# Second cross attention begun inside the block of the rotary projection, in the rotations' buffers

## The chip, the cores and the metric

The kernel runs on one core of a Trainium2 chip. The metric is device time in microseconds (us) of one execution of the whole program; lower is better. Five instruction streams run beside each other and meet only at semaphores: TensorE (PE: matmuls, and PEld: its weight loads), VectorE (DVE), ScalarE (ACT), GpSimd (POOL) and SyncE (SP), which issues most of the DMA transfers.

## The reference

Two layers work on x, 16 batches of 64 rows of 256. Each layer is a cross attention against a context of 128 keys per batch, a self attention and a feed-forward stage. The cross attention of the second layer, whose start is changed, is this (16 heads, latent width 192, key width 64):

```python
q_hk  = (hidden_q @ Wq.T).reshape(b, s, H, K)
q_big = jnp.einsum('bshk,hkq->bshq', q_hk, w_kc_q)     # then rotated by position in this layer
q_r   = jnp.einsum('bshq,hqr->bhsr', q_big, W_qr)
k_r   = jnp.einsum('bld,hdr->bhlr', kv_rope, W_kr)
attn  = softmax(einsum('bhsr,bhlr->bhsl', q_r, k_r))
ctx_c = einsum('bhsl,bld->bhsd', attn, kv_rope)
out   = einsum('bhsd,hkd->bshk', ctx_c, w_kc_kv).reshape(b, s, H * K) @ Wo.T
```

## The kernel before

Every stage is a function that opens a block: an area of the program in which each engine has its own instruction list, written out by hand, and at whose end all engines meet. Buffers that a block allocates are free again after it. The order of work on an engine is the order in its list; nothing is rescheduled.

**Projection, `cross_project_rotary` (L1498).** The queries are made in 24 steps k: four quads of four heads, each for two halves of the batches (half 0 is batches 0 to 7, half 1 is 8 to 15; the pair is a unit, so there are units 0 to 7), three chunks of the latent each. Per step, PE makes two products `big(k, 0)` and `big(k, 1)`, DVE multiplies each by a table of cosines or sines (`rotate`, L1769: two 128x1024 products, into `times_a[k % 2]` and `times_b[k % 2]`), POOL adds the two (L1553, into `turned[k % 3]`), and PE folds the sum into the latent banks 6 and 7 (`fold(k)`, L1644 and L1652), two steps behind its own `big`. After the third chunk of a unit, ACT rounds the query to fp16 (`high`, L1714) and DVE subtracts for the low part (`low`, L1780, which counts the semaphore `q_lo` up by 4 a unit). ACT and POOL also split weights of the coming self attention in the last six steps (`split_rotary_*`, `split_output_*`, four slices of the output weight at L1828 and L1835). The last two folds, the last `high` and the last `low` come after the loop.

**Attention, `cross_attention` (L584), used by both layers.** A block of its own, with its own buffers. It walks over tiles of two batches; `j` is the batch whose scores are made, `b` the one two batches behind. For one batch:

- PE `score(j)` (L643): 16 matmuls into two banks of one pair (pairs alternate with j);
- DVE `neg_max` (L800): two reductions, one for each half of the heads (q = 0, 1);
- ACT `exponentials` (L717): eight activations that also give the row sums, four for each q;
- DVE `invert` (L771): one reciprocal for each q;
- POOL normalises the probabilities (L753), one instruction for each q, and copies the keys (L749);
- PE `turn` (L640) transposes them, DVE copies them out (`probs_t`, L786), PE `mix` (L658) multiplies by the keys, ACT rounds (`ctx_hi`, L730), DVE subtracts (`ctx_lo`, L775); after two batches PE `output` (L672) makes the output product, DVE adds it to x (L810).

On DVE the order within batch j is: copy of turn q = 0, invert(j-1, 0), `ctx_lo`, copy of turn q = 1, invert(j-1, 1), then the two maxima of j. So maxima of j are queued behind the last reciprocal of j-1, which waits for the last exponential of j-1.

Of the kernel before, what the change touches and what calls it, by code (L numbers as in the profile page):

```python
# [14 lines left out]
ALU = mybir.AluOpType  # L15
# [7 lines left out]
P = 128  # L23
# [7 lines left out]
BH = B // 2  # L31
# [326 lines left out]
def cross_project_plain(nc, g):  # L358
# [4 lines left out]
    with ExitStack() as own:  # L363
# [185 lines left out]
        def _(dve):  # L549
# [31 lines left out]
            pair_loop(step)  # L581


def cross_attention(nc, g, tag, weights=None):  # L584
# [13 lines left out]
    HP = PAIRS // 2  # L598
    with ExitStack() as own:  # L599
        def sb(name, shape, dt):  # L600
            return own.enter_context(nc.sbuf_tensor(f"{tag}_{name}", shape, dt))

        probs = [sb(f"probs{u}", [P, PAIRS, L], F32) for u in range(2)]
        probs_t = [sb(f"probs_t{u}", [P, PAIRS, P], F32) for u in range(2)]
        keys = [sb(f"keys{u}", [P, DC], F32) for u in range(2)]
        ctx_hi = [sb(f"ctx_hi{v}", [P, PAIRS, 2, S], F16) for v in range(2)]
        ctx_lo = [sb(f"ctx_lo{v}", [P, PAIRS, 2, S], F16) for v in range(2)]
        neg_max = [sb(f"neg_max{u}", [P, PAIRS], F32) for u in range(2)]
        total = [sb(f"total{u}", [P, PAIRS], F32) for u in range(2)]
        inverse = [sb(f"inverse{u}", [P, PAIRS], F32) for u in range(2)]  # L610
        scored, maxed, exped = g.sem(f"{tag}_scored"), g.sem(f"{tag}_maxed"), g.sem(f"{tag}_exped")
        inverted, normed = g.sem(f"{tag}_inverted"), g.sem(f"{tag}_normed")
        turned, turn_kept = g.sem(f"{tag}_turned"), g.sem(f"{tag}_turn_kept")
        keys_kept = g.sem(f"{tag}_keys")
        mixed, mix_high, mix_kept = g.sem(f"{tag}_mixed"), g.sem(f"{tag}_mix_high"), g.sem(f"{tag}_mix_kept")
        out_done, added = g.sem(f"{tag}_out"), g.sem(f"{tag}_added")

        ln = normalise_steps(nc, g, f"{tag}_ln", groups=[(2 * q, 2 * q + 2) for q in range(TILES // 2)])
        score_bank = [[g.bank[k][:].rearrange("p (n l) -> p n l", n=HP) for k in banks]
                      for banks in ((0, 1), (6, 7))]  # L620
        turn_bank = [g.bank[k][:].rearrange("p (n l) -> p n l", n=HP) for k in (2, 3)]
        mix_bank = g.bank[4][:]
        out_bank = [g.bank[k][:, 0:D] for k in (5,) * (TILES - 2) + (0, 1)]
        mix_view = mix_bank.rearrange("p (n s) -> p n s", n=PAIRS)
        block = own.enter_context(nc.Block())

        SCALED = (5, 7)

        def tile_loop(eng, step):
            for i in range(TILES + 3):  # L630
                step(i, i % 2, i < TILES, 1 <= i <= TILES, 2 <= i <= TILES + 1)

        @block.tensor
        def _(pe):
            def turn(b, u):
                for q in range(2):
                    pe.wait_ge(normed, 2 * b + q + 1)
                    wait(pe, turn_kept, 2 * b + q - 1)
                    for n in range(HP):
                        mm = nc.tensor.transpose(turn_bank[q][:, n, :], probs[u][:, q * HP + n, :], m.ident[:])  # L640
                    mm.then_inc(turned, 1)

            def score(j, u):  # L643
                for q in range(2):
                    wait(pe, exped, 2 * j + q - 3)
                    for n in range(HP):
                        at = 2 * (q * HP + n)
                        lhs = m.q_stack[:, j, at:at + 2, :]
                        mm = accumulate(nc, score_bank[u][q][:, n, :],
                                        [(lhs, m.kvt_hi[:, j, :]), (lhs, m.kvt_lo[:, j, :])])  # L650
                    mm.then_inc(scored, 1)

            def mix(b, u):
                pe.wait_ge(turn_kept, 2 * b + 2)
                pe.wait_ge(keys_kept, b + 1)
                wait(pe, mix_kept, b)
                for e in range(2):
                    mm = nc.tensor.matmul(mix_view[e * DC:(e + 1) * DC], keys[u][:],  # L658
                                          probs_t[u][:, :, e * S:(e + 1) * S], start=True, stop=True)
                mm.then_inc(mixed, 1)  # L660

            def output(t, u):
                v = t % 2
                if u == 0:
                    pe.wait_ge(mix_kept, 2 * t + 2)
                    if t < TILES - 2:
                        wait(pe, added, t)
                for n in range(u * HP, (u + 1) * HP):
                    hi, lo = (c[v][:, n, :, :].rearrange("p b s -> p (b s)") for c in (ctx_hi, ctx_lo))
                    factors = split_factors(hi, lo, m.out_hi[:, n, :], m.out_lo[:, n, :])  # L670
                    for k, (lhs, rhs) in enumerate(factors):
                        mm = nc.tensor.matmul(out_bank[t], lhs, rhs, start=(n == 0 and k == 0),  # L672
                                              stop=(n == PAIRS - 1 and k == len(factors) - 1))
# [1918 lines left out]
```

## Time and profile before

| what | value |
|---|---|
| time, median of 3 runs | 779.67 us (778.89 to 780.49) |
| the profiled execution's own time | 774.19 us |
| span of the profiled execution | 772.4 us |
| mean granted TensorE clock | 0.954 |
| PE, DVE, ACT, POOL busy | 89%, 76%, 54%, 50% of the span |
| changed seam: last `low` of the projection to first score of the attention | about 415 us from the span's start |

A timeline row gives the start, the duration (of a merged run of instructions, where x is over 1), the engine, the line, what is written and read, and in brackets how long the engine stood idle before it and what released it. A windows row gives for a stretch the busy time of each engine and the clock that was granted to TensorE (1.00 is 2.4 GHz, 0.50 is 1.2 GHz).

### The profile page before, as it was taken

What the parts mean: (1) busy time and instruction counts of PE and PEld (TensorE: products, weight loads), DVE (VectorE), ACT (ScalarE), POOL (GpSimd) and SP (SyncE); (2) the same over time, 40 slices, a digit from 0 to 9 for tenths busy, and PEclk for the clock granted to TensorE, in tenths of its full rate; (3) what the DMA queues carried; (4) which work ended last, traced back from release to release, by engine and by line L of the source; (5) the groups of instructions that cost most, each with busy time, mean ns of one, the idle gap of its engine ahead of it and who ended that gap; (6) DMA issues with size and microseconds to landing.
All of it is one profiled execution on the core that took longest, in us unless ns stands there. A gap on an engine that the chain in (4) does not pass through costs nothing. (4 is left out here: it accounts for less than half of the span.)

```text
span 772.4 us, 15774 instructions
## 1 busy us (share of the span) xinstructions
PE 685.5 (89%) x5490; PEld 462.7 (60%) x5490; DVE 584.1 (76%) x1149; ACT 418.9 (54%) x1317; POOL 384.8 (50%) x338
## 2 busy tenths in 40 slices
PE   5997899998767489999995999889999999999987
PEld 4664677687424354445333677567777776767754
DVE  4466789765788765757684899897888888889787
ACT  2565778654358422222335878255555656566575
POOL 1503555473146324434485555356576687777512
PEclk9998899998579589999998999999999999999999
DMA  6465000000110041710010000023331221211001
GB/s 195 132 188 220 1 3 1 1 2 1 59 38 1 0 140 38 239 54 1 1 41 1 2 2 2 1 62 98 117 111 46 62 62 44 62 43 42 2 0 57
DMA packets 33576, 41.97 MB, mean 54 GB/s; under 512 B 15073, under 2 KB 23265, under 8 KB 32609
## 3 DMA queue, kind: packets, MB, share of 16 engines
q1 hardware_dynamic: 33504, 41.06, 17.4%
q8 instruction: 40, 0.66, 0.3%
q14 instruction: 32, 0.25, 0.1%
HBM read 40.00 MB, written 1.05 MB: 53 GB/s over the span
## 5 line engine op out<-in xcount | busy, mean ns | idle before, releaser
L2140 POOL TENSOR_TENSOR ra_direct<-ra_direct,ra_crossed 128x512 f32<-128x512 f32 x64 | 81.2, 1270 | 73.6 <-DVE ra_crossed L2326 73.5
L717 ACT ACTIVATE c_probs<-bank,c_neg_max 128x128 f32<-128x128 f32 x256 | 91.2, 382 | 29.4 <-DVE c_neg_max L800 29.4
L2326 DVE SCALAR_TENSOR_TENSOR ra_crossed<-bank,ra_bias,ra_sin 64x512 f32<-64x512 f32 x128 | 96.0, 750 | 1.9
L753 POOL TENSOR_TENSOR c_probs<-c_probs,c_inverse 128x512 f32<-128x512 f32 x64 | 66.6, 1041 | 61.1 <-DVE c_inverse L771 61.1
L1553 POOL TENSOR_TENSOR r_turned<-r_times_a,r_times_b 128x1024 f32<-128x1024 f32 x24 | 56.4, 2351 | 70.6 <-DVE r_times_b L1769 70.6
L2275 ACT ACTIVATE ra_probs_t<-bank 64x256 f32<-64x256 f32 x64 | 24.2, 378 | 60.4 <-PE bank L2214 60.1
L717 ACT ACTIVATION_READ_ACCUMULATOR c_probs<-bank,c_neg_max 128x1 f32 x256 | 56.5, 221 | 0.0
L2283 ACT ACTIVATE ra_probs<-ra_masked,ra_neg_max 128x64 f32<-128x64 f32 x128 | 42.9, 336 | 20.0 <-DVE ra_neg_max L2346 19.7
L1850 POOL TENSOR_TENSOR ra_w_lo<-ra_raw,ra_w_hi 128x768 f16<-128x768 f32 x32 | 52.7, 1647 | 0.0
L58 PE MATMUL bank<-xt_hi,ra_w_hi 128*128 128x512 f16 x128 | 49.1, 384 | 0.9 <-PEq L599 0.9
L58 PE MATMUL bank<-xt_hi,ra_w_lo 128*128 128x512 f16 x128 | 49.0, 383 | 0.0
L58 PE MATMUL bank<-xt_lo,ra_w_hi 128*128 128x512 f16 x128 | 49.0, 383 | 0.0
L2326 DVE SCALAR_TENSOR_TENSOR ra_direct<-bank,ra_bias,ra_cos 128x512 f32<-128x512 f32 x64 | 47.5, 743 | 1.0 <-PE bank L58 0.7
L786 DVE COPY c_probs_t<-bank 128x512 f32<-128x512 f32 x64 | 43.8, 684 | 5.6 <-PE bank L640 5.2
L2374 DVE SCALAR_TENSOR_TENSOR ra_z_lo<-bank,ra_v_bias,ra_z_hi 128x512 f16<-128x512 f32 x32 | 23.9, 748 | 29.4 <-ACT ra_z_hi L2296 29.4
L640 PEld LDWEIGHTS bank<-ident_sb,c_probs 128*128 128x128 f32 x256 | 28.6, 145 | 28.4 <-issue 21.1
L58 PE MATMUL bank<-ra_w_hi,xt_hi 128*128 128x128 f16 x256 | 44.9, 220 | 0.0
L58 PE MATMUL bank<-ra_w_lo,xt_hi 128*128 128x128 f16 x256 | 44.9, 220 | 0.0
L58 PE MATMUL bank<-ra_w_hi,xt_lo 128*128 128x128 f16 x256 | 44.9, 220 | 0.0
L800 DVE TENSOR_REDUCE c_neg_max<-bank 128x4 f32<-128x512 f32 x64 | 40.9, 678 | 2.6 <-PE bank L58 2.5
L58 PE MATMUL bank<-kvt_hi,l_q_stack 128*128 128x128 f16 x256 | 35.8, 233 | 7.5 <-PEq L1508 4.5
L640 PE MATMUL bank<-ident_sb,c_probs 128*128 128x128 f32 x256 | 36.9, 287 | 3.6 <-POOL c_probs L753 3.6
(271 smaller groups left out, 2082.0 us busy)
## 6 DMA issues: line engine op xcount, KB each, us to landing
ra_raw<-l_attn_w_dram SPq DMA_DIRECT2D x32, 384.0 KB, 3.0
wq<-l_wq_dram SPq DMA_DIRECT2D x16, 256.0 KB, 2.8
wo<-l_wo_dram SPq DMA_DIRECT2D x16, 256.0 KB, 3.4
wkcq<-l_wkcq_dram SPq DMA_DIRECT2D x16, 192.0 KB, 2.8
ra_wo<-l_attn_wo_dram SPq DMA_DIRECT2D x1, 2048.0 KB, 10.7
wqr<-l_wqr_dram SPq DMA_DIRECT2D x16, 96.0 KB, 2.3
wkv<-l_wkv_dram SPq DMA_DIRECT2D x16, 64.0 KB, 2.8
x_res<-x_dram SPq DMA_DIRECT2D x2, 512.0 KB, 5.6
```

Of the source, the lines that this page charges most:

```text
L58: mm = nc.tensor.matmul(out, lhs, rhs, start=(n == 0), stop=(n == last))
L640: mm = nc.tensor.transpose(turn_bank[q][:, n, :], probs[u][:, q * HP + n, :], m.ident[:])
L717: e = nc.scalar.activation(probs[u][:, n, :], score_bank[u][q][:, n - q * HP, :], ACT.Exp, bias=neg_max[u][:, n:n + 1], accum_out=total[u] ...
L753: nc.gpsimd.tensor_tensor(out=probs[u][:, at, :], in0=probs[u][:, at, :], in1=inverse[u][:, at].unsqueeze(2).broadcast_to([P, HP, L]), op= ...
L786: nc.vector.tensor_copy(probs_t[u][:, at, :], turn_bank[q]).then_inc(turn_kept, 1)
L800: nc.vector.tensor_reduce(neg_max[u][:, at], score_bank[u][q], AX.X, ALU.max, negate=True).then_inc(maxed, 1)
L1553: nc.gpsimd.tensor_tensor(out=turned[k % 3][:], in0=times_a[k % 2][:], in1=times_b[k % 2][:], op=ALU.add).then_inc(rotated, 1)
L1850: nc.gpsimd.tensor_tensor(out=m.ra_w_lo[f][:], in0=m.ra_raw[f % 2][:], in1=m.ra_w_hi[f][:], op=ALU.subtract).then_inc(g.ra_split, 1)
L2140: nc.gpsimd.tensor_tensor(out=direct[e][k][:], in0=direct[e][k][:], in1=crossed[k][:], op=ALU.add).then_inc(roped, 1)
L2275: ins = nc.scalar.activation(probs_t[at, :, b, :], turn_bank[at].rearrange("p (a s) -> p a s", a=TH), ACT.Copy)
L2283: ins = nc.scalar.activation(probs[1 - e][:, t, :], masked[1 - e][:, t, :], ACT.Exp, bias=neg_max[1 - e][:, t:t + 1], scale=-1.0, accum_ou ...
L2326: ins = nc.vector.scalar_tensor_tensor(dst[out_lo:out_lo + rows].rearrange("p t (b s) -> p (t b) s", b=2), src[lo:lo + rows], bias[e][lo:l ...
```

## The change

The attention becomes a set of steps, `cross_attention_steps`, that can be put into another block. The first layer uses it as before in a block of its own (with a few waits more on PE, on semaphores that have passed). In the second layer the block is gone: the projection's block runs the attention's steps on each engine.

- PE: `score(0)` before fold 22, `score(1)` before fold 23 (both need only half 0 of the queries), then the rest from the turn of batch 0.
- ACT: the eight exponentials of batch 0 before the last two `high`, then the rest from batch 1.
- DVE: the maxima of batch 0 after the last rotation; then the attention's list, with the last `low` of side 0 after the maxima of batch 1 and that of side 1 after the maxima of batch 2.
- POOL: the fourth slice of `split_output_low` moves from behind the last rotation to behind the normalising of batch 1.
- Buffers: the probabilities, their transposes and the contexts lie in the rotations' buffers. Banks: scores (3, 4) and (0, 1), turns 2 and 5, mix 6, output 7. PE waits for the last `low` of side 0 before the first mix (bank 6) and for that of side 1 before the first output (bank 7).

```diff
-def cross_attention(nc, g, tag, weights=None):
+def cross_attention_steps(nc, g, own, tag, banks, ready, room=None, weights=None):
...
+    even, odd, turns, mixes, outs = banks
+    ln = normalise_steps(nc, g, f"{tag}_ln", groups=[(2 * q, 2 * q + 2) for q in range(TILES // 2)],
+                         banks=odd + (6, 7))
...
+    queries, first_ready, all_ready = ready
...
+    def score(pe, j):
+        u = j % 2
+        if j in (0, BH):
+            pe.wait_ge(queries, first_ready if j == 0 else all_ready)
...
+        def mix(b, u):
+            pe.wait_ge(turn_kept, 2 * b + 2)
+            pe.wait_ge(keys_kept, b + 1)
+            wait(pe, mix_kept, b)
+            if b == 0 and begun:
+                pe.wait_ge(queries, all_ready - 2)
...
+                if t == 0:
+                    pe.wait_ge(queries, all_ready)
...
+                if head and j >= begun:
+                    score(pe, j)
...
+                if head and j >= begun:
+                    exponentials(act, j, 0)
...
+                for q in range(2):
+                    at = slice(q * HP, (q + 1) * HP)
+                    pool.wait_ge(inverted, 2 * j + q + 1)
+                    nc.gpsimd.tensor_tensor(
+                        out=probs[u][:, at, :], in0=probs[u][:, at, :],
+                        in1=inverse[u][:, at].unsqueeze(2).broadcast_to([P, HP, L]),
+                        op=ALU.mult).then_inc(normed, 1)
+                if u == 0 and i in SCALED:
+                    ln.rstd(pool, SCALED.index(i))
+                between(j)
...
+                if head and j >= begun:
+                    peak(dve, j)
+                if i < 2:
+                    between(j)
...
@@ -1537,7 +1581,20 @@
+        room = {"probs": [sb("probs0", [P, PAIRS, L])[:], wide(times_a[0])],
+                "probs_t": [wide(times_b[0]), wide(times_a[1])],
+                "ctx_hi": contexts(times_b[1]), "ctx_lo": contexts(turned[0])}
         ln = g.ln1
+        att = cross_attention_steps(nc, g, own, "c1", ((3, 4), (0, 1), (2, 5), 6, 7), (q_lo, 4 * (UNITS - 1), 4 * UNITS),
+                                    room)
...
-                elif at >= 2:
+                elif 2 <= at < PER_QUAD - 1:
                     split_output_low(nc, g, pool, at - 2)
+
+            def between(j):
+                if j == 1:
+                    split_output_low(nc, g, pool, 3)
+
+            att.gpsimd(pool, between)
...
-            for k in (STEPS - 2, STEPS - 1):
+            for j, k in enumerate((STEPS - 2, STEPS - 1)):
+                if j == 1:
+
+                    pe.wait_ge(multiplied, 2 * STEPS - 1)
+                att.score(pe, j)
                 fold(k)
+            pe.wait_ge(multiplied, 2 * STEPS)
+            att.tensor(pe, 2)
...
+            for q in range(2):
+                att.exponentials(act, 0, q)
             for side in range(2):
                 high(UNITS - 1, side)
+            att.scalar(act, 1)
...
-            for side in range(2):
-                low(UNITS - 1, side)
+            att.peak(dve, 0)
+
+            def between(j):
+                if j in (1, 2):
+                    low(UNITS - 1, j - 1)
+
+            att.vector(dve, 1, between)
+    return att.ln
...
-            cross_project_rotary(nc, g)
-            ln = cross_attention(nc, g, "c1")
+            ln = cross_project_rotary(nc, g)
```

## Rows read from the trace of the kernel before

**Rows 1.** The page: span, and busy time, share and instructions of each engine.
```profile
span 772.4 us, 15774 instructions
PE 685.5 (89%) x5490; PEld 462.7 (60%) x5490; DVE 584.1 (76%) x1149; ACT 418.9 (54%) x1317; POOL 384.8 (50%) x338
```

**Rows 2.** Windows: stretch, length, busy PE, PEld, DVE, ACT, POOL; clock; DMA share, GB/s.
```profile
404.00:410.00 6.00, 3.28 (x10) 1.15 (x12) 1.66 (x2) 0.00 (x0) 6.00 (x4) 1.00 0.00 0
...
415.00:420.00 5.00, 3.45 (x34) 3.31 (x35) 1.75 (x5) 4.19 (x17) 1.28 (x2) 0.72 0.02 5
...
435.00:440.00 5.00, 5.00 (x49) 3.77 (x47) 4.29 (x9) 4.16 (x24) 2.92 (x4) 1.00 0.02 5
```

**Rows 3.** Timeline of PE at the seam.
```profile
403.59 0.38 PE L58 MATMUL bank<-xt_hi,r_big_lo 128*128 128x512 f16 x1
404.31 1.98 PE L1652 MATMUL bank<-r_turned,r_fold_outer 128*128 128x512 f32 x4 [0.34 <-POOL r_turned L1553]
408.70 1.93 PE L1644 MATMUL bank<-r_turned,r_fold_inner 64*64 64x512 f32 x8 [2.40 <-POOL r_turned L1553]
415.10 0.27 PE L58 MATMUL bank<-kvt_hi,l_q_stack 128*128 128x128 f16 x1 [4.46 <-PEq L1508]
```

**Rows 4.** Timeline of DVE at the seam.
```profile
401.86 1.41 DVE L1780 TENSOR_TENSOR l_q_stack<-bank,l_q_stack 64x512 f16<-64x512 f32 x2
...
404.44 1.21 DVE L1769 TENSOR_TENSOR r_times_b<-bank,r_table_b 128x1024 f32<-128x1024 f32 x1
411.92 2.85 DVE L1780 TENSOR_TENSOR l_q_stack<-bank,l_q_stack 64x512 f16<-64x512 f32 x4 [6.27 <-ACT l_q_stack L1714]
```

**Rows 5.** Timeline of POOL at the seam and in batches 1 and 2.
```profile
406.30 2.35 POOL L1553 TENSOR_TENSOR r_turned<-r_times_a,r_times_b 128x1024 f32<-128x1024 f32 x1
408.59 2.14 POOL L1835 TENSOR_TENSOR ra_wo_lo<-ra_wo,ra_wo_hi 128x1024 f16<-128x1024 f32 x1
...
423.80 1.04 POOL L753 TENSOR_TENSOR c_probs<-c_probs,c_inverse 128x512 f32<-128x512 f32 x1 [0.36 <-DVE c_inverse L771]
...
426.80 1.04 POOL L753 TENSOR_TENSOR c_probs<-c_probs,c_inverse 128x512 f32<-128x512 f32 x1 [1.16 <-DVE c_inverse L771]
```

**Rows 6.** Timeline of ACT: seam, then the first exponential of batches 0, 1, 2, 3, 8.
```profile
410.68 2.44 ACT L1714 ACTIVATE l_q_stack<-bank 64x512 f16<-64x512 f32 x4 [8.42 <-PE bank L1644]
415.06 1.28 ACT L717 ACT_TABLE_LOAD   x1 [1.93 <-PEq L1508]
416.87 0.37 ACT L717 ACTIVATE c_probs<-bank,c_neg_max 128x128 f32<-128x128 f32 x1 [0.53 <-DVE c_neg_max L800]
...
420.60 0.37 ACT L717 ACTIVATE c_probs<-bank,c_neg_max 128x128 f32<-128x128 f32 x1 [0.82 <-DVE c_neg_max L800]
...
424.35 0.37 ACT L717 ACTIVATE c_probs<-bank,c_neg_max 128x128 f32<-128x128 f32 x1 [0.84 <-DVE c_neg_max L800]
...
428.59 0.37 ACT L717 ACTIVATE c_probs<-bank,c_neg_max 128x128 f32<-128x128 f32 x1 [0.85 <-DVE c_neg_max L800]
...
449.75 0.37 ACT L717 ACTIVATE c_probs<-bank,c_neg_max 128x128 f32<-128x128 f32 x1 [0.84 <-DVE c_neg_max L800]
```

**Rows 7.** Lines of 425 to 475 us: busy, mean ns, idle before and its releaser.
```profile
L717 ACT ACTIVATE c_probs<-bank,c_neg_max 128x128 f32<-128x128 f32 x95 | 33.9, 383 | 9.2 <-DVE c_neg_max L800 9.2
```

**Rows 8.** Timeline of DVE from the maxima of batch 2 to those of batch 3.
```profile
423.63 1.27 DVE L800 TENSOR_REDUCE c_neg_max<-bank 128x4 f32<-128x512 f32 x2
425.94 0.69 DVE L786 COPY c_probs_t<-bank 128x512 f32<-128x512 f32 x1 [1.03 <-PE bank L640]
...
427.89 1.26 DVE L800 TENSOR_REDUCE c_neg_max<-bank 128x4 f32<-128x512 f32 x2
```

**Rows 9.** Windows: the start of the first layer's attention.
```profile
73.10:83.20 10.10, 8.68 (x55) 6.15 (x53) 5.76 (x12) 7.57 (x41) 4.55 (x6) 0.50 0.00 1
```

**Rows 10.** Timeline of ACT there: first exponential of batches 2 and 3.
```profile
81.38 0.37 ACT L717 ACTIVATE c_probs<-bank,c_neg_max 128x128 f32<-128x128 f32 x1 [0.84 <-DVE c_neg_max L800]
86.37 0.37 ACT L717 ACTIVATE c_probs<-bank,c_neg_max 128x128 f32<-128x128 f32 x1 [1.42 <-DVE c_neg_max L800]
```

More of the change, by code:

```diff
@@ new lines, in sb, with taken @@
+    def sb(name, shape, dt):
+        return own.enter_context(nc.sbuf_tensor(f"{tag}_{name}", shape, dt))
+    def taken(name, count, shape, dt):
+        return room[name] if room and name in room else [sb(f"{name}{u}", shape, dt)[:] for u in range(count)]
+    probs = taken("probs", 2, [P, PAIRS, L], F32)
+    probs_t = taken("probs_t", 2, [P, PAIRS, P], F32)
+    keys = [sb(f"keys{u}", [P, DC], F32) for u in range(2)]
+    ctx_hi = taken("ctx_hi", 2, [P, PAIRS, 2, S], F16)
+    ctx_lo = taken("ctx_lo", 2, [P, PAIRS, 2, S], F16)
@@ new lines, in gpsimd, with step @@
+    def gpsimd(pool, between=lambda j: None):
+        def step(i, v, head, middle, tail):
+            if not head:
+                return
+            for u in range(2):
+                j = 2 * i + u
+                wait(pool, mixed, j - 1)
+                nc.gpsimd.tensor_copy(keys[u][:], m.kv2[:, j, 0, :]).then_inc(keys_kept, 1)
+                for q in range(2):
+                    at = slice(q * HP, (q + 1) * HP)
[7 more added lines that the diff above has]
+                between(j)
+        if weights:
+            weights.fill_ones(pool)
+        tile_loop(step)
+        ln.rstd(pool, 2)
@@ L625, in cross_attention @@
+    att = Fields()
+    att.score, att.exponentials, att.peak, att.ln = score, exponentials, peak, ln
+    att.tensor, att.scalar, att.gpsimd, att.vector = tensor, scalar, gpsimd, vector
+    return att
+def cross_attention(nc, g, tag, banks, ready, weights=None):
+    with ExitStack() as own:
+        att = cross_attention_steps(nc, g, own, tag, banks, ready, None, weights)
         block = own.enter_context(nc.Block())
[L627 to L631, printed above, removed]
@@ L653, in mix @@
[L653 to L673, printed above, removed]
-                if u == 1:
-                    mm.then_inc(out_done, 1)
@@ L690, in step @@
-            def step(i, v, head, middle, tail):
-                for u in range(2):
-                    j, b = 2 * i + u, 2 * i + u - 2
-                    if middle:
-                        turn(b, u)
-                    if head:
-                        score(j, u)
-                    if u and tail and i < TILES + 1:
-                        output(i - 2, 0)
-                    if not u and 3 <= i < TILES + 2:
-                        output(i - 3, 1)
-                    if middle:
-                        mix(b, u)
-                    if middle and not head:
-                        pe.wait_ge(exped, 2 * B - 1 + u)
-                        ln.transpose(pe, u)
-                    if u and i == TILES + 1:
-                        last_output()
@@ L722, in step @@
-            def step(i, v, head, middle, tail):
-                for u in range(2):
-                    j, b = 2 * i + u, 2 * i + u - 2
-                    if head:
-                        exponentials(j, u, 0)
-                    if middle:
-                        act.wait_ge(mixed, b + 1)
-                        wait(act, out_done, i - 2)
-                        nc.scalar.activation(ctx_hi[1 - v][:, :, u, :], mix_view, ACT.Copy).then_inc(mix_high, 1)
-                    if head:
-                        exponentials(j, u, 1)
-                    if middle and not head:
-                        ln.high(act, u)
```

320 lines of the change are left out of this document (177 added, 143 removed).

## The prediction

> **What bounds the kernel now.** I began with the page. TensorE is busy for 89% of the span and no other engine for more than 76% [rows 1], which says little of a seam between two stages. So I read windows around it: of the 6 us from 404 us on PE works 3.28, DVE 1.66 and ACT nothing (only POOL is busy), while in the steady attention PE fills its window entirely [rows 2]. The seam is a chain of waits, and I read it engine by engine from the timelines.
>
> The chain is: POOL makes the last rotated sum until 408.65 [rows 5]; PE folds it, 408.70 to 410.63 [rows 3]; ACT rounds the last queries, 410.68 to 413.12 [rows 6]; DVE makes their low parts, 411.92 to 414.77 [rows 4]; then all engines meet at the end of the block and the first score starts at 415.10 [rows 3]. The first exponential comes at 416.87 [rows 6], because a maximum lies before it. The table load at 415.06 (1.28 us) is over at 416.34 and costs nothing [rows 6]. All the while batches 0 to 7 have been ready: their last low part, of unit 6, ends at 403.27 [rows 4]. That is the slack which the change can reach, from the front.
>
> What sets the pace behind the seam decides whether a head start is kept. The first exponentials of batches 3 and 8 lie 21.16 us apart [rows 6], 4.23 us a batch. Between 425 and 475 us all of the 9.2 us for which the exponentials waited were ended by the maxima [rows 7]. So the pace is a loop: exponentials of j, reciprocal, maxima of j+1 (queued behind it on DVE), exponentials of j+1. The loop has no tie to a fixed point in time, and no transfer is in it. PE's work fits into this period, but only just [rows 2].
>
> **The change, step by step.** I follow one marker, the first exponential of batch 3, since from there on the loop repeats. It stands at 428.59 now [rows 6].
>
> *Scores 0 and 1.* PE issues its last `big` product at 403.59 and waits 0.34 us for fold 22 [rows 3]. In the window from 415 on, the 32 matmuls of two scores and two more take 3.45 us [rows 2], so a score is at most 1.7 us at a mostly low clock; from 404 to 410 the clock is 1.00 [rows 2], and my estimate there is half of it, 0.9 us. Score 0 runs at about 403.9 to 404.8, fold 22 moves behind it by some 0.6 us and ends at about 406.9, score 1 is done before 408. Fold 23 waits for POOL until 408.65 in any case, after 2.40 us of idle time [rows 3]. Both scores are hidden in that idle time; without it they would cost 1.8 us, and with the low clock they would push fold 23 by 0.6 us. Score 1 needs bank 1, whose rotation is the one before that of 404.44, so it is free by then [rows 4]. Price: nothing.
>
> *Maxima and exponentials of batch 0.* DVE is idle for 6.27 us after the last rotation (404.44 + 1.21 = 405.65) [rows 4]: maxima until 406.9. ACT is idle for 8.42 us before 410.68 [rows 6]. The table load fits ahead of the first exponential (ACT is free from 410.68 - 8.42 = 402.26), the eight exponentials take 2.9 us (batch 0 begins at 416.87, and batch 1 begins at 420.60 after 0.82 us of idle time [rows 6]: 419.78 less 416.87). They run at about 406.4 to 409.3, before the last fold ends at 410.63. `high` starts at 410.68 as before. Price: nothing; if the cover were gone, `high` would be late by what they pass 410.68; there are 1.4 us to spare. The copies behind exponentials need no new table load: the attention has this mix already, and its starts are evenly 4.23 us apart [rows 6].
>
> *Batch 1.* Its maxima are queued behind the reciprocals of batch 0 (409.4), and end at about 410.7, before `low` of side 0 can start at 411.92 [rows 4]. Its exponentials come behind `high` on ACT: 413.1. POOL normalises batch 0 from 408.65 on; it no longer has the fourth slice (2.14 us) there [rows 5]. PE turns batch 0 and makes score 2 by 412.7.
>
> *Batch 2.* Now batch 1 starts at 420.60 and batch 2 at 424.35, 3.75 us later [rows 6]. Nothing in that step is new: reciprocal 1, then maxima 2. 413.1 + 3.75 = 416.85, which is **7.50 us earlier** than 424.35.
>
> *Low part of side 1.* It stands on DVE behind the maxima of batch 2, and the copy of turn 1, the reciprocals and maxima of batch 3 are queued behind it. The maxima of batch 2 end 0.55 us after the marker of batch 2 (423.63 + 1.27 = 424.90 against 424.35) [rows 6, 8], so at 417.4. Half of the 2.85 us row [rows 4] is 1.43: 418.8. From the copy to the start of the maxima of batch 3 it is 1.95 us (425.94 to 427.89), and 0.70 from there to the exponential (428.59) [rows 6, 8]: 418.8 + 1.95 + 0.70 = 421.45. Without it, the loop would give 416.85 + 4.24 = 421.09. So it costs about 0.4 of its 1.43 us, and the rest takes the place of 1.03 us for which DVE waits there now [rows 8]. The mix of batch 0 waits for the low part of side 0, which ends at about 413.3; the copies that it also needs come after it. The output of tile 0 comes two batches later.
>
> *Fourth slice on POOL.* The second normalising of batch 1 starts 3.20 us after that batch's marker (423.80 against 420.60) [rows 5, 6]: 416.3 to 417.3; the slice 2.14 us [rows 5]: 419.5. Behind it on POOL is the key copy and the first normalising of batch 2, now 2.45 us after its marker (426.80 against 424.35) [rows 5, 6], which would be 419.3, and about 419.5 with DVE's delay above. So it is late by 0.2 us, and PE's turn waits for it; DVE's copy of that turn comes only after the maxima of batch 3, about 422.0. Bounds: 0 and 2.14; I take 0, by the rows, since the turn is ready before DVE is.
>
> *The first layer.* It gets three waits on PE for semaphores that have passed, tens of ns at the most; and a block end goes, which is in the marker's way already (414.77 to 415.10). Price: nothing.
>
> **Sum:** 428.59 - 421.45 = **7.1 us**. Against the profiled execution's 774.19 that is 767.1. It lies 5.5 us below the median of 779.67. Nothing on the seam's chain is a transfer or differs by chance as far as these rows show, so I take the 7.1 us from the median as well: **772.6**, 0.9% less.
>
> **TensorE's clock.** At the seam PE idles 4.46 us [rows 3], and the window from 415 on has a mean clock of 0.72, that is partly 1.2 GHz [rows 2]. In the first layer, the attention's start runs wholly at 0.50 for 10 us, busy for 8.68 of 10.10 us [rows 9], and there batches 2 and 3 are 4.99 us apart (86.37 less 81.38) and not 4.23 [rows 10]: the low clock costs 0.76 us, once. Here the 4.46 us gap goes, but PE becomes sparse between 412.7 and 421 (turn, mix and one score each in some 4 us). The Trainium skill (TensorE: Matmul & The Clock Gate, Part 4: PE-mode transpose) says that transposes do not count as busy time for the clock gate; by it half of that work would not count, and the sum would be 7.1 - 0.8 = 6.3 us. No row here separates transposes from other matmuls. I take 0, because the gap that precedes the low clock now is gone, and keep 0.8 as a rival.
>
> **Rivals.**
> - *The clock falls in the sparse start* and costs what it costs in the first layer, 0.76 us: 773.4. For it: the first layer's start [rows 9, 10]. Against: the long gap is gone, and the loop is set by ACT and DVE, so only a PE that is very late shows. The skill's sentence on transposes stands on this side.
> - *The moved pieces queue wholly*: the low part with 1.43 instead of 0.4, and the slice with 2.14 us. 7.5 - 1.43 - 2.14 = 3.9: 775.8. For it: both stand in the loop's lists. Against: the idle 1.03 us before the copy, and POOL's idle 1.16 us before the normalising [rows 5, 8].
> - *The head start is given back or the seam was hidden*: 779.7. It would need something behind the seam that is bound to a fixed time, a transfer for instance. The timeline of ACT and its releasers show none [rows 6, 7].
> - *Slower: TensorE stays at 1.2 GHz in the steady attention.* PE's work fills its window at full clock [rows 2], so a batch would take up to twice 4.23, 4.2 us more. Two such batches eat the 7.1 us, three make it 12.7 - 7.1 = 5.6 us slower: 785.3. Trigger: the clock falls in the sparse start and doesn't rise. Against: in the first layer it rose by itself after 83.2, before the outputs begin, since PE at the low clock was busy nearly all the time [rows 9].
>
> **How the numbers follow.** Forecast 0.65, clock 0.18, queueing 0.10, no gain 0.04, slower 0.03. About 0.2% (1.6 us) is what a measurement of this kernel can tell from no change. Faster by more than that: the first three, 0.93; within it 0.04; slower 0.03. The range starts at 779.67 less 7.5 (the low part free) less 1.6 for the scatter of the runs (they span 1.6 us): 770.5. It goes up to 776.0, which takes in the clock and the queueing case (775.8), and leaves out the last two, 0.07. What is left of the 0.2 is for prices that I have not thought of.
>
> **What would show it.** Right: score 0 and 1 between the last `big` and fold 23; exponentials of batch 0 before the last `high`, which stays at 410.7; batch 1 at 413.1, batch 2 near 416.9, batch 3 near 421.5, then 4.23 us a batch; the last low part of 1.43 us between maxima 2 and the copy of turn 1. Wrong: fold 23 or `high` later than now; a second table load; batch 3 later than 422.2 (clock) or 423.5 (queueing); the period above 4.23; a stage after the attention that is longer than before.

## The result, and the profile after

| | before | changed |
|---|---|---|
| time, median | 779.28 us (16 runs, 775.5 to 783.81) | 770.53 us (16 runs, 767.58 to 776.13) |
| ratio | 1 | 0.9895, 95% interval 0.9872 to 0.9918 |
| the profiled execution | 774.19 us, span 772.4 | 769.27 us, span 767.4 |

The ratio means 8.2 us less (6.4 to 10.0). Forecast were 7.1 us less and a time of 772.6 us; measured were 770.53. A second series of the same two kernels gave a ratio of 0.9906 (0.9874 to 0.9938), which is 7.3 us.

The two spans differ by 5.0 us only, and that is not the size of the effect at the seam. The last rotation of the projection ends at 405.65 us in the trace of before [rows 4] and at 407.80 in the changed one: 2.15 us that lie ahead of the seam. That is scatter: in three traces of the kernel before, this point lies anywhere between 405.65 and 411.13 us. So everything below is measured from the end of the last rotation (T), up to the first product of the self attention, 493.02 before and 488.75 after. That stretch went from 87.37 to 80.95 us, 6.42 us less. What follows it took 279.38 and 278.65 us.

PE in the changed kernel:

```profile
405.73 0.38 PE L58 MATMUL bank<-xt_hi,r_big_lo 128*128 128x512 f16 x1
405.95 0.22 PE L58 MATMUL bank<-kvt_hi,l_q_stack 128*128 128x128 f16 x1
...
406.84 1.94 PE L1715 MATMUL bank<-r_turned,r_fold_outer 128*128 128x512 f32 x4
408.62 0.22 PE L58 MATMUL bank<-kvt_hi,l_q_stack 128*128 128x128 f16 x1
...
410.86 1.93 PE L1707 MATMUL bank<-r_turned,r_fold_inner 64*64 64x512 f32 x8 [1.18 <-POOL r_turned L1610]
412.72 1.09 PE L657 MATMUL bank<-ident_sb,r_probs 128*128 128x128 f32 x8
...
417.65 1.08 PE L667 MATMUL bank<-r_times_b,c_keys 128*64 128x512 f32 x4 [2.94 <-DVE r_times_b L805]
...
423.08 1.63 PE L667 MATMUL bank<-r_times_a,c_keys 128*64 128x512 f32 x4 [1.94 <-DVE r_times_a L805]
424.64 1.97 PE L657 MATMUL bank<-ident_sb,r_probs 128*128 128x128 f32 x8
```

Score 0 takes 0.89 us (405.95 to 406.84) and stands between the last `big` and fold 22 (L1715). Score 1 begins at 408.62, behind fold 22. Fold 23 (L1707) still waits for POOL, now for 1.18 us and not 2.40 [rows 3], so both scores are hidden. The turn of batch 0 follows at once. The names `r_times_b`, `r_times_a` and `r_probs` are only the new places of the attention's data, in the projection's block.

ACT in the changed kernel: table load, first exponential of batch 0, the last `high`, first exponentials of batches 1, 2, 3, 4 and 9:

```profile
404.42 1.28 ACT L727 ACT_TABLE_LOAD   x1
408.43 0.37 ACT L727 ACTIVATE r_probs<-bank,c_neg_max 128x128 f32<-128x128 f32 x1 [2.73 <-DVE c_neg_max L781]
...
412.84 2.44 ACT L1783 ACTIVATE l_q_stack<-bank 64x512 f16<-64x512 f32 x4 [1.51 <-PE bank L1707]
415.31 0.37 ACT L727 ACTIVATE r_times_a<-bank,c_neg_max 128x128 f32<-128x128 f32 x1
...
419.04 0.37 ACT L727 ACTIVATE r_probs<-bank,c_neg_max 128x128 f32<-128x128 f32 x1 [0.84 <-DVE c_neg_max L781]
...
423.72 0.37 ACT L727 ACTIVATE r_times_a<-bank,c_neg_max 128x128 f32<-128x128 f32 x1 [1.29 <-DVE c_neg_max L781]
...
428.44 0.37 ACT L727 ACTIVATE r_probs<-bank,c_neg_max 128x128 f32<-128x128 f32 x1 [1.34 <-DVE c_neg_max L781]
...
449.56 0.37 ACT L727 ACTIVATE r_times_a<-bank,c_neg_max 128x128 f32<-128x128 f32 x1 [0.84 <-DVE c_neg_max L781]
```

From the `high` on, the steps are 3.73 us (batch 1 to 2), 4.68 (2 to 3), 4.72 (3 to 4), then 4.22 a batch ((449.56 - 428.44) / 5). Two of them are longer than the period, and the brackets show where it goes: ACT waits 1.29 and 1.34 us for the maxima instead of 0.84. Each of the two has its own cause. DVE:

```profile
407.72 1.28 DVE L781 TENSOR_REDUCE c_neg_max<-bank 128x4 f32<-128x512 f32 x2
...
411.46 1.26 DVE L781 TENSOR_REDUCE c_neg_max<-bank 128x4 f32<-128x512 f32 x2
414.08 1.41 DVE L1852 TENSOR_TENSOR l_q_stack<-bank,l_q_stack 64x512 f16<-64x512 f32 x2 [1.36 <-ACT l_q_stack L1783]
...
419.64 1.41 DVE L1852 TENSOR_TENSOR l_q_stack<-bank,l_q_stack 64x512 f16<-64x512 f32 x2
421.08 0.69 DVE L805 COPY r_times_a<-bank 128x512 f32<-128x512 f32 x1
...
423.03 1.26 DVE L781 TENSOR_REDUCE c_neg_max<-bank 128x4 f32<-128x512 f32 x2
425.80 0.69 DVE L805 COPY r_times_b<-bank 128x512 f32<-128x512 f32 x1 [1.51 <-PE bank L657]
```

Between the maxima of batch 2 and those of batch 3 (423.03) DVE is never idle: its own list, with the low part at 419.64, is what is long. Ahead of those of batch 4 it waits 1.51 us for PE's turn. And PE was slow there, as the windows show (length, busy PE, PEld, DVE, ACT, POOL, clock):

```profile
421.10:423.00 1.90, 0.04 (x1) 0.00 (x0) 1.90 (x5) 1.33 (x8) 1.74 (x3) 1.00 0.00 0
423.50:426.40 2.90, 2.90 (x12) 1.70 (x9) 1.39 (x3) 2.68 (x14) 0.97 (x2) 0.50 0.00 0
```

Behind an idle stretch on PE the granted clock is 0.50 (1.2 GHz), over the mix of batch 1 and the first eight transposes of batch 2: 1.97 us for the transposes at 424.64, which take 1.09 at 412.72. POOL, last, has the moved slice (L1913) ahead of the normalising of batch 2:

```profile
408.47 2.34 POOL L1610 TENSOR_TENSOR r_turned<-r_times_a,r_times_b 128x1024 f32<-128x1024 f32 x1
...
419.49 2.13 POOL L1913 TENSOR_TENSOR ra_wo_lo<-ra_wo,ra_wo_hi 128x1024 f16<-128x1024 f32 x1
421.57 0.24 POOL L759 COPY c_keys<-kv 128x64 f32<-128x64 f32 x1
421.93 1.04 POOL L763 TENSOR_TENSOR r_probs<-r_probs,c_inverse 128x512 f32<-128x512 f32 x1
```

POOL is done with the slice and the key copy behind it at 421.81, and starts the normalising at 421.93. The reciprocal that this needs comes behind the copy at 421.08 on DVE. The slice is just out of the way.

### The profile page after: what moved, and what is told of

Its sections match the earlier page's. It is cut to its first block and busy times, and to the rows that moved or that the text cites. A ratio compares the mean times of both kernels' runs of the same rounds, so it can differ in the third digit from the quotient of the medians.

```text
span 767.4 us, 15768 instructions
## 1 busy us (share of the span) xinstructions
PE 681.0 (89%) x5490; PEld 459.1 (60%) x5490; DVE 583.6 (76%) x1149; ACT 418.3 (55%) x1317; POOL 384.7 (50%) x338
## 5 line engine op out<-in xcount | busy, mean ns | idle before, releaser
L727 ACT ACTIVATE c_probs<-bank,c_neg_max 128x128 f32<-128x128 f32 x128 | 45.5, 382 | 16.0 <-DVE c_neg_max L781 16.0
L763 POOL TENSOR_TENSOR c_probs<-c_probs,c_inverse 128x512 f32<-128x512 f32 x32 | 33.3, 1040 | 31.0 <-DVE c_inverse L790 31.0
L258 DVE TENSOR_TENSOR l_q_stack<-bank,l_q_stack 64x512 f16<-64x512 f32 x32 | 22.0, 689 | 23.7 <-ACT l_q_stack L250 23.2
L1841 DVE TENSOR_TENSOR r_times_a<-bank,r_table_a 128x1024 f32<-128x1024 f32 x24 | 29.3, 1221 | 13.7 <-PE bank L58 13.5
L1841 DVE TENSOR_TENSOR r_times_b<-bank,r_table_b 128x1024 f32<-128x1024 f32 x24 | 29.3, 1221 | 13.4 <-PE bank L58 13.1
L109 POOL TENSOR_TENSOR all_rstd<-all_var,minus_half 128x2 f32<-128x2 f32 (+3 forms) x16 | 12.8, 799 | 49.4 <-DVE all_var L103 35.9
L58 PE MATMUL bank<-kvt_hi,l_q_stack 128*128 128x128 f16 x256 | 33.6, 226 | 3.0 <-PEq L363 3.0
```

The source lines that it names most:

```text
L58: mm = nc.tensor.matmul(out, lhs, rhs, start=(n == 0), stop=(n == last))
L727: e = nc.scalar.activation(probs[u][:, n, :], score_bank[u][q][:, n - q * HP, :], ACT.Exp, bias=neg_max[u][:, n:n + 1], accum_out=total[u] ...
L763: nc.gpsimd.tensor_tensor(out=probs[u][:, at, :], in0=probs[u][:, at, :], in1=inverse[u][:, at].unsqueeze(2).broadcast_to([P, HP, L]), op= ...
L1841: nc.vector.tensor_tensor((times_a, times_b)[w][k % 2][:].rearrange("p t (b s) -> p t b s", b=BH), src, (table_a, table_b)[w][:, c].unsque ...
```

## The experiments

The trace of each kernel is reduced to the same markers. All times are in us from T, the end of the last rotation, except the last column, which runs from the first product of the self attention to the end of the span. "Batch j" is its first exponential.

| kernel | fold 23, duration | batch 1 | batch 2 | batch 3 | batch 4 | self attention | rest |
|---|---|---|---|---|---|---|---|
| before | 3.05, 1.93 | 14.95 | 18.70 | 22.94 | 27.17 | 87.37 | 279.38 |
| before_again | 3.05, **3.63** | 16.63 | 20.37 | 24.59 | 28.81 | 88.92 | 277.90 |
| before_third | 3.02, 1.93 | 14.91 | 18.65 | 22.87 | 27.09 | 87.23 | 280.74 |
| before_last_fold_filled | 3.06, 1.93 | 14.97 | 18.71 | 22.95 | 27.17 | 87.37 | 277.55 |
| one_block_only | 3.04, 1.93 | 14.77 | 18.51 | 22.76 | 26.99 | 87.19 | 278.42 |
| late_exponentials | 3.04, 1.93 | 12.65 | 16.40 | 20.63 | 24.86 | 85.06 | 280.22 |
| changed | 3.06, 1.93 | 7.51 | 11.24 | 15.92 | 20.64 | 80.95 | 278.65 |
| after_again | 3.06, 1.93 | 7.50 | 11.24 | 15.92 | 20.14 | 80.25 | 279.18 |
| low_together | 3.07, 1.93 | 7.51 | 11.25 | 15.47 | 19.70 | 79.82 | 278.95 |
| splits_in_gap | 2.47, 1.93 | 6.92 | 10.66 | 15.35 | 19.92 | 80.22 | 281.77 |
| gaps_filled | 3.05, 1.93 | 7.50 | 11.24 | 15.93 | 20.16 | 80.36 | 277.65 |
| four_more_early | 3.05, 1.93 | 4.36 | 10.56 | 15.24 | 19.47 | 79.68 | 280.99 |
| combined | 2.47, 1.93 | 4.35 | 10.53 | 15.52 | 19.75 | 79.88 | 279.83 |
| transposes_long | 3.05, 1.93 | 7.50 | 11.24 | 20.97 | 25.20 | 85.40 | 279.32 |

**before_again, after_again, before_third: the same two kernels again.** No edit.

> The kernel before, unchanged. It shows what the comparison gives where nothing differs, and how the stretches ahead of and behind the seam differ between executions. I measure three stretches: span start to the start of fold 23 (408.70 us in the trace of before, 410.86 in that of the changed kernel), fold 23 to the first product of the self attention (84.32 before, 77.89 changed: 6.43 us less), and from there to the end (279.4 and 278.7). Theory A (the seam gives all of the gain, the rest of the difference is scatter of the other stretches): the middle stretch is 84.3 again within 0.3, the outer ones differ by a few us. Theory B (the change also moved something outside the seam): the outer stretches are steady to 0.5 us in repeated executions of the same kernel.

> The changed kernel, unchanged. Theory A: middle stretch 77.9 us, or 77.4 if the clock does not fall at batch 3; outer stretches scattered like those of before. Theory B: first stretch again near 410.9 and last again near 278.7.

> The kernel before once more, for a third look at fold 23: 1.93 us at full clock or 3.63 at 1.2 GHz, with a middle stretch of 84.3 or 85.9. If its clock is low again, that is the common case; at 1.93 the two of three traces agree with the prediction's rows.

Timed: before_again against before 0.9974 (0.9946 to 1.0001), so a ratio off by 0.26% is what nothing gives here; after_again 0.9906 (0.9874 to 0.9938). The rest behind the seam scatters between 277.9 and 280.7 us with the kernel before, and T itself between 405.65 and 411.13: theory A. But the stretch of the seam was not steady either. In before_again fold 23 took 3.63 us:

```profile
411.93 3.63 PE L1644 MATMUL bank<-r_turned,r_fold_inner 64*64 64x512 f32 x8 [2.40 <-POOL r_turned L1553]
```

and the windows ahead of it and over it are

```profile
409.50:411.90 2.40, 0.03 (x1) 0.00 (x0) 0.00 (x0) 0.00 (x0) 2.40 (x3) 1.00 0.00 0
411.90:415.60 3.70, 3.63 (x8) 0.75 (x8) 0.00 (x0) 0.00 (x0) 2.05 (x1) 0.54 0.00 0
```

The fold is on the chain, and the seam is 1.55 us longer for it (88.92 against 87.37). In the other two traces of before it ran at 1.00.

After_again shows a fall of the clock at another place, at the mix and the turn of batches 0 and 1:

```profile
418.22 1.96 PE L667 MATMUL bank<-r_times_b,c_keys 128*64 128x512 f32 x4 [2.94 <-DVE r_times_b L805]
...
423.64 1.08 PE L667 MATMUL bank<-r_times_a,c_keys 128*64 128x512 f32 x4 [0.80 <-DVE r_times_a L805]
```

The mix took 1.96 us and not 1.08, and no marker moved: batch 3 at T + 15.92 as in the changed kernel, batch 4 after 4.22 us. DVE was at the maxima of batch 2 and the low part then (418.90 to 421.61) and came to the copies only at 421.64. So in this trace a fall one batch earlier cost nothing.

**before_last_fold_filled: is it the idle time ahead of fold 23?** Nine products that nobody waits for fill part of it: PE is idle for 0.41 us ahead of the fold, not 2.40.

```diff
             for k in (STEPS - 2, STEPS - 1):
+                if k == STEPS - 1:
+                    for _ in range(9):
+                        nc.tensor.matmul(g.bank[3][:, 0:P], m.ident[:], m.ident[:], start=True, stop=True)
                 fold(k)
```

> The kernel before with nine 128x128 products of the identity on PE between fold 22 and fold 23, where it is idle for 2.4 us; nobody waits for them. In one of two traces of the kernel before, fold 23 ran at 1.2 GHz: 3.63 us and not 1.93, with the middle stretch 85.9 and not 84.3. Theory: the idle time ahead of the fold lets the clock fall, and the changed kernel, which has the scores there, is spared it (that is worth up to 1.7 us in some executions, on top of the seam's 6.4). Then fold 23 takes 1.93 us here, middle stretch 84.3, and the median is below that of before by the mean of it, some 0.5 us, which the timing can't tell. Rival: the fall has nothing to do with that idle time; then 3.63 can come here as well. One trace can refute the theory and not prove it.

Fold 23 at full clock, stretch 87.37; time 0.9979 (0.9952 to 1.0006). It agrees with the theory and does not prove it, as two of three traces without the filling look the same. The timing says only that filling the gap is worth less than 0.5% (3.7 us).

**one_block_only: the block's end by itself.** Everything in one block and in the new buffers, nothing early: PE makes folds 22 and 23 and then `att.tensor(pe)`, ACT both `high` and then `att.scalar(act)`, DVE both `low` and then `att.vector(dve)`, POOL its fourth slice where it was, and the first score waits for all queries:

```diff
-        att = cross_attention_steps(nc, g, own, "c1", ((3, 4), (0, 1), (2, 5), 6, 7), (q_lo, 4 * (UNITS - 1), 4 * UNITS),
+        att = cross_attention_steps(nc, g, own, "c1", ((3, 4), (0, 1), (2, 5), 6, 7), (q_lo, 4 * UNITS, 4 * UNITS),
...
-                att.score(pe, j)
...
-            att.tensor(pe, 2)
+            att.tensor(pe)
...
-            for q in range(2):
-                att.exponentials(act, 0, q)
...
-            att.peak(dve, 0)
...
-                if j in (1, 2):
-                    low(UNITS - 1, j - 1)
+            for side in range(2):
+                low(UNITS - 1, side)
+            att.vector(dve)
```

> The attention runs in the projection's block and buffers, but nothing of it is early: both folds, both roundings, both low parts first, then score 0. If the head start of the work is what counts, the middle stretch is that of before less the meeting of the engines, 0.3 us, so 84.0, and the time is the same within noise. The rival is that the block's end itself cost more (fetching of instructions, the table load at the block's start): then the middle stretch is below 83 us.

1.0016 (0.9989 to 1.0043); batch 3 0.18 us earlier than before. So the meeting of the engines costs 0.2 us, and the new buffers and the waits added to the first layer, which this kernel has too, gain nothing that the timing could tell. The table load now comes right behind `high` at 417.17 and is still hidden behind the maxima.

**late_exponentials: the head start without ACT's part.** Scores 0 and 1 and the maxima of batch 0 stay early; both low parts go ahead of the rest of DVE's list.

```diff
-            for q in range(2):
-                att.exponentials(act, 0, q)
             for side in range(2):
                 high(UNITS - 1, side)
+            for q in range(2):
+                att.exponentials(act, 0, q)
             att.scalar(act, 1)
...
-            def between(j):
-                if j in (1, 2):
-                    low(UNITS - 1, j - 1)
-            att.vector(dve, 1, between)
+            for side in range(2):
+                low(UNITS - 1, side)
+            att.vector(dve, 1)
```

> As the changed kernel, but the exponentials of batch 0 come behind the last rounding on ACT, and both low parts before the reciprocals of batch 0 on DVE. Scores 0, 1 and the maxima of batch 0 stay early. If ACT is what the head start hangs on: exponentials of batch 0 at fold 23 + 4.4, batch 1 at + 8.2, batch 2 at + 11.9, batch 3 at + 16.1 (12.86 in the changed kernel, 19.89 in that of before), middle stretch 80.5, about 3.8 us faster than before. If early scores and maxima alone were enough, it stays near 78.

0.9953 (0.9924 to 0.9983), batch 3 2.31 us earlier than before and 4.71 later than in the changed kernel. Batch 3 came at fold 23 + 17.59 (16.1 was expected). ACT shows what accounts for 1.28 of the 1.49 us that I was off:

```profile
417.64 2.44 ACT L1783 ACTIVATE l_q_stack<-bank 64x512 f16<-64x512 f32 x4 [8.43 <-PE bank L1707]
420.10 1.28 ACT L727 ACT_TABLE_LOAD   x1
421.40 0.37 ACT L727 ACTIVATE r_probs<-bank,c_neg_max 128x128 f32<-128x128 f32 x1
```

The load of 1.28 us stands on the chain as soon as the maxima are ready in time. The changed kernel has it at 404.42, ahead of the exponentials and in ACT's idle time.

**low_together: the price of the low part behind maxima 2.**

```diff
             def between(j):
-                if j in (1, 2):
-                    low(UNITS - 1, j - 1)
+                if j == 1:
+                    for side in range(2):
+                        low(UNITS - 1, side)
```

> As the changed kernel, but the last low part of side 1 follows that of side 0 on DVE, ahead of the copies of turn 0, and no longer stands behind the maxima of batch 2. It measures what that piece costs where the change put it. Theory of the prediction (it costs 0.4 us there, since DVE's list from the copy of turn 1 to the maxima of batch 3 starts late): from batch 2 to batch 3 it is 4.25 us and not 4.68, and batch 3 stands at fold 23 + 12.4. Rival (that step is late for another reason: POOL's slice or PE's turn of batch 1): it stays at 4.7.

The step from batch 2 to 3 went from 4.68 to 4.22 us, batch 2 stayed at T + 11.25, time 0.9911 (0.9877 to 0.9944). DVE: both low parts in one piece, and a wait of 0.47 us ahead of the copy of turn 1 again.

```profile
414.42 2.85 DVE L1852 TENSOR_TENSOR l_q_stack<-bank,l_q_stack 64x512 f16<-64x512 f32 x4 [1.36 <-ACT l_q_stack L1783]
...
418.67 1.27 DVE L781 TENSOR_REDUCE c_neg_max<-bank 128x4 f32<-128x512 f32 x2
420.41 0.69 DVE L805 COPY r_times_a<-bank 128x512 f32<-128x512 f32 x1 [0.47 <-PE bank L657]
```

So the low part cost 0.46 us where the change put it. POOL's slice was still in its place here; it has no share in the 4.68.

**splits_in_gap: POOL's slices.**

```diff
-                elif 2 <= at < PER_QUAD - 1:
+                elif 2 <= at < PER_QUAD - 2:
                     split_output_low(nc, g, pool, at - 2)
...
-                if j == 1:
-                    split_output_low(nc, g, pool, 3)
+                if j == 0:
+                    for q in (2, 3):
+                        split_output_low(nc, g, pool, q)
```

> As the changed kernel, but POOL makes the third and the fourth slice of the output weight's low part after the normalising of batch 0, where it is idle for 3.95 us; the third no longer stands before the last rotated sum. If the last sum waits for that slice (it starts 408.47 in the changed kernel, the rotation ended at 407.8), fold 23 comes 0.7 us earlier, measured from the end of the last rotation, and the normalising of batch 2 starts with its reciprocal. The two slices take 4.3 us in a gap of 3.95 us, so the first normalising of batch 1 may be late by 0.3 us. Batch 3 at fold 23 + 12.9 as before, or + 12.5 if POOL's slice, not DVE's low part, is what makes the step to batch 3 long.

The third slice no longer stands ahead of POOL's last sum. Fold 23 came 2.47 and not 3.06 us after T, and batches 1, 2 and 3 0.6 us earlier from T. The step from 2 to 3 is still 4.69. Time 0.9899 (0.9853 to 0.9946). The clock fell again ahead of batch 4 (step 4.57): the mix of batch 1 took 1.48 us at 427.11.

**gaps_filled: does the idle PE bring the fall?**

```diff
-                mm = accumulate(nc, score_bank[u][q][:, n, :],
-                                [(lhs, m.kvt_hi[:, j, :]), (lhs, m.kvt_lo[:, j, :])])
+                for _ in range(3 if room and j == 3 else 1):
+                    mm = accumulate(nc, score_bank[u][q][:, n, :],
+                                    [(lhs, m.kvt_hi[:, j, :]), (lhs, m.kvt_lo[:, j, :])])
...
+            if begun and b == 0:
+                pe.wait_ge(queries, all_ready - 2)
+                for _ in range(9):
+                    nc.tensor.matmul(mix_bank[:, 0:P], m.ident[:], m.ident[:], start=True, stop=True)
```

> As the changed kernel, with work added on PE that nobody waits for: nine 128x128 products of the identity ahead of the first mix, and the products of score 3 made three times over. They fill the two idle stretches on PE (2.9 and 1.9 us) ahead of the place where the clock fell to 1.2 GHz in the trace of the changed kernel and batch 4 came 4.72 us after batch 3. Clock theory: granted clock 1.00 from fold 23 to the end of the attention, batch 4 4.23 us after batch 3, middle stretch 77.3. Rival (the fall is not tied to those idle stretches): 0.50 somewhere there again in this execution, or the step is 4.7 at full clock. A repeated execution of the changed kernel without filling had 4.22 there too, so one trace with a clock of 1.00 can only agree.

From fold 23 on, over 27 us:

```profile
412.90:440.00 27.10, 24.86 (x238) 17.83 (x239) 21.53 (x43) 20.87 (x101) 15.79 (x20) 1.00 0.01 2
```

Clock 1.00 throughout, step from batch 3 to 4 4.23, time 0.9884 (0.9851 to 0.9918). What the expectation says of the repeated execution holds for its step of 4.22, but its clock had fallen too, a batch earlier. Of the six unfilled traces with the exponentials of batch 0 early, four had a fall in this stretch (changed, after_again, splits_in_gap, combined) and two had none (low_together, four_more_early). The two filled ones, this and transposes_long, had none. So the clean filled trace agrees with the theory and does not prove it.

**transposes_long: do transposes count?**

```diff
+            if begun and b == 0:
+                pe.wait_ge(queries, all_ready - 2)
+                for _ in range(80):
+                    nc.tensor.transpose(mix_bank[:, 0:P], m.ident[:], m.ident[:])
             pe.wait_ge(turn_kept, 2 * b + 2)
```

> As the changed kernel, with 80 transposes of the identity on PE ahead of the first mix, some 9 us in which PE does nothing else. The attention is some 7 us later for it. The question is only what the granted clock does in that stretch. If transposes don't count as work for the clock, it falls to 0.50 within the stretch or just behind it, although PE is busy throughout, and a transpose then takes longer than 0.116 us apart. If they count, it stays at 1.00.

One execution, 780.3 us. The stretch with nothing but transposes on PE:

```profile
421.50:430.30 8.80, 8.78 (x80) 8.72 (x80) 4.18 (x8) 4.19 (x24) 4.18 (x3) 1.00 0.00 0
```

The clock stayed at 1.00 for 8.8 us and behind it, 0.11 us for a transpose. It was at 1.00 when they began, so this shows that they kept it, not that they would raise a low one. The cost was 5.1 us against after_again (85.40 less 80.25) and not 7, as part of the stretch lay in PE's idle time.

**four_more_early and combined: can it be beaten?** Four_more_early:

```diff
             for q in range(2):
                 att.exponentials(act, 0, q)
+            att.exponentials(act, 1, 0)
             for side in range(2):
                 high(UNITS - 1, side)
-            att.scalar(act, 1)
+            att.exponentials(act, 1, 1)
+            att.scalar(act, 2)
```

Combined is this and the edit of splits_in_gap.

> As the changed kernel, but the first four exponentials of batch 1 also come ahead of the last rounding on ACT, which is idle there for 1.5 us. If ACT's list sets batch 2, it starts 0.7 us earlier, at fold 23 + 7.45 (8.18 in the changed kernel), and batch 3 at + 12.15, since the low part behind the maxima of batch 2 still costs its 0.46. The price is that the last rounding starts 0.9 us late. Rival: the low part of side 0 comes late by that and holds the copies of turn 0 and with them the reciprocals, so that batch 2 stays at 8.2.

> The changed kernel with two edits that the traces point to: the four exponentials more ahead of the last rounding, and both output weight slices of POOL after batch 0's normalising. Fold 23 0.6 us earlier, measured from the end of the last rotation; batch 2 at fold 23 + 7.45, batch 3 at + 12.15. In all 1.3 us less than the changed kernel, ratio to before about 0.988; the difference to the changed kernel is smaller than what the timed runs can tell, so the markers decide. Rival: POOL is late with the normalising of batch 1 by the second slice, and batch 3 stays at 12.9.

Four_more_early did it: batch 2 at T + 10.56 and batch 3 at T + 15.24, 0.68 us earlier than in the changed kernel; time 0.9909 (0.9881 to 0.9937). Combined has fold 23 at T + 2.47, but batch 2 at T + 10.53: nothing on top. The last `high` is no longer held by the fold. It comes right behind the exponentials on ACT, 1.33 us after the end of fold 23 (413.89), and these hang on T:

```profile
415.22 2.44 ACT L1784 ACTIVATE l_q_stack<-bank 64x512 f16<-64x512 f32 x4
```

Then the clock fell, at T + 9.8 as in after_again, but with batch 2 now 0.7 us earlier:

```profile
419.31 1.98 PE L667 MATMUL bank<-r_times_b,c_keys 128*64 128x512 f32 x4 [3.36 <-DVE r_times_b L805]
421.21 1.78 PE L657 MATMUL bank<-ident_sb,r_times_a 128*128 128x128 f32 x8
```

The step to batch 3 was 4.99 us, and 4.68 in four_more_early, which had no fall. Its time is 0.9920 (0.9900 to 0.9940). No version was shown faster than the changed kernel: the intervals of low_together, splits_in_gap, gaps_filled, four_more_early and combined overlap with its own, 0.9872 to 0.9918, and gains of 0.4 to 0.7 us at the marker of batch 3 are below what the timing can tell.

## Why the prediction was right

**The chain at the seam: right.** Fold 23 and `high` stand where they did from T. Fold 23 at T + 3.05 before and T + 3.06 after.

**Scores, maxima, exponentials of batch 0 at no price: right.** 0.89 us a score as estimated; fold 22 moved by 0.38 us from T, where 0.6 was said; exponentials at 408.43 (0.63 after T) and done before `high` at 412.84 with 1.51 us to spare (1.4 said).

**The markers.** From T the sum gave batch 1 at 7.45 us, batch 2 at 11.20, batch 3 at 15.80; they came at 7.51, 11.24 and 15.92. So batch 3 gained 7.02 us where 7.14 was said. How much of it hangs on ACT is shown by late_exponentials, which gets 2.31 of the 7.02; of the 4.71 that it lacks, 1.28 are the table load. One_block_only gets 0.18.

**The low part: 0.46 us where 0.4 was said**, by low_together. POOL's slice costs nothing behind batch 1, as taken: without it there the step from batch 2 to 3 is still 4.69 us (splits_in_gap). What it costs ahead of the last sum (0.6 us, splits_in_gap) was no part of the change, since the third slice was there in both.

**The clock: the step that I took at 0.** The rival, at 0.18, had 0.76 us. In the trace of the changed kernel it happened, and cost 0.49 us at once (4.72 against 4.23). The stretch from the first exponential of batch 15 to the self attention is 13.85 us there, against 13.64 before and 13.66 in after_again. DVE waits for two late turns of PE in it:

```profile
476.11 0.69 DVE L805 COPY r_times_b<-bank 128x512 f32<-128x512 f32 x1 [0.31 <-PE bank L657]
...
480.35 0.69 DVE L805 COPY r_times_a<-bank 128x512 f32<-128x512 f32 x1 [0.26 <-PE bank L657]
```

In after_again the same two copies follow without a wait. The eleven steps between batches 4 and 15 were 0.10 us shorter than before, at the quicker pace told of at the end. So 7.02 - 0.49 - 0.21 + 0.10 = 6.42. That PE never made up what the fall had cost it, and so was late at the end as well, fits (its work only just fills the period; splits_in_gap, with a fall at the same place, has 13.75), but was not tested. If it is so, the fall cost 0.70 us in that execution, close to the rival's 0.76. In after_again the clock fell a batch earlier, and that cost nothing. The argument "the gap that precedes the low clock is gone" was wrong in form: 4.46 us of idle time went, but stretches of 2.94 and 1.94 us came, and falls followed them in some executions and not in others. The Trainium skill (TensorE: Matmul & The Clock Gate, Part 4: PE-mode transpose) says that transposes do not count as busy time for the clock gate. The runs do not bear that out: 80 transposes in a row kept the granted clock at the 1.00 that it had when they began (transposes_long).

**What was missing: the clock in the kernel before.** I took fold 23 as 1.93 us from one trace. Four traces have 2.4 us of idle time on PE ahead of it (before, before_again, before_third, one_block_only), and in one of them it ran at 1.2 GHz, on the chain. In all nine traces with the scores in that gap it took 1.93, and so it did with the gap filled. The mean stretch of three traces of before is 87.84 (87.37, 88.92, 87.23), that of two of the changed kernel 80.60 (80.95, 80.25): 7.24 us, against 8.2 (6.4 to 10.0) timed. The 1 us between the two lies within the interval and is not explained. That the scores keep the clock up for fold 23 fits every trace here, but how often it falls without them stays open with so few.

**The rest behind the seam** did not take the gain back: 279.38, 277.90, 280.74 before, 278.65, 279.18 after. The rivals "given back" and "slower" are out, as the timed interval leaves at least 6.4 us of gain. The clock was back at 1.00 for the steady attention, from T + 32 to T + 80 us, in all fourteen traces.

**The range: met by luck.** Its lower end is 770.5, and the measured median is 770.53. For the scatter it allowed 1.6 us, the span of three runs; sixteen runs of the same kernel span 8.3 us (775.5 to 783.81). The mechanism and the 7.1 us do not hang on this, but a range made this way was too narrow.

## What to carry to other kernels

When a loop with its own period starts behind a chain of waits, ask what of it can start before the chain ends, and count the gain at one marker in the loop, step by step; here that was good to 0.1 us. Measure such a seam from its own start: the stretches ahead and behind scatter by more than the effect. Look for idle stretches of TensorE ahead of work on the chain, and read more than one trace before you take a clock for granted.

## What the runs showed of the hardware that was not expected

- The same fold took 1.93 or 3.63 us in executions of one kernel, after the same 2.40 us of idle time on PE [rows 3].
- A fall of the clock for some 3 us cost 0.49 us at the next batch in the changed kernel and nothing in after_again. In before_third the clock was 0.50 over most of the attention's start, where in before it was back at 1.00 in between, and the markers stood within 0.1 us of those in before:

```profile
420.50:429.50 9.00, 7.59 (x58) 6.70 (x60) 4.91 (x11) 7.08 (x33) 3.80 (x6) 0.50 0.01 3
```

- The loop's period, which ACT and DVE set, is 4.23 us in some executions and 4.22 in others of the same kernel, at a granted clock of 1.00. From batch 3 to batch 8 it is 21.16 us in before [rows 6] and 21.12 in before_third:

```profile
434.00 0.37 ACT L717 ACTIVATE c_probs<-bank,c_neg_max 128x128 f32<-128x128 f32 x1 [0.84 <-DVE c_neg_max L800]
...
455.12 0.37 ACT L717 ACTIVATE c_probs<-bank,c_neg_max 128x128 f32<-128x128 f32 x1 [0.84 <-DVE c_neg_max L800]
```

That is 0.2%, about as much as a timed ratio can tell of this kernel. It goes with the execution and not with the kernel: of three executions of the kernel before, one has 4.23 and two have 4.22. What differs between such executions was not tried.
